# A post-norm transformer layer on one core: four FFN groups walked back and forth, the last block's norm inside the FFN, first loads on two queues

## The reference

```python
q, k, v = (x @ w.T + b).reshape(B, S, 32, 16)        # for wq, wk, wv
scores  = einsum('bshd,bstd->bsht', q, k) / 4          # 32 x 32 for each token
context = einsum('bsht,bstd->bshd', softmax(scores), v)
x = layernorm(x + context)
dq = nf4_dequant(nf4_quant(w))                         # w1, w2 [1376, 512], w3 [512, 1376]
h = silu(x @ dq1.T) * (x @ dq2.T)
x = layernorm(x + h @ dq3.T)
```

## Time and profile before

| what | value |
|---|---|
| median of three executions | 825.99 us |
| profiled execution | 828.94 us, span 827.1 us |
| PE, DVE, ACT, POOL busy | 738.1, 631.5, 469.5, 112.5 us |
| granted clock of TensorE, mean | 0.85 of full speed |
| HBM read, written | 80.55 MB, 38.80 MB |

### The profile page before, as it was taken

The page is one execution under the profiler, slowest core; times in us unless marked ns, Lnnn a source line. Parts: engine busy times, 40 slices in busy tenths (PEclk is TensorE's granted clock), DMA queues, the critical chain, the costliest instruction groups (busy, mean ns, idle before and its releaser), DMA issues.

```text
span 827.1 us, 14113 instructions
## 1 busy us (share of the span) xinstructions
PE 738.1 (89%) x5668; PEld 629.3 (76%) x5668; DVE 631.5 (76%) x844; ACT 469.5 (57%) x599; POOL 112.5 (14%) x91
## 2 busy tenths in 40 slices
...
GB/s 190 248 123 96 189 129 160 138 233 243 252 186 247 139 273 151 246 250 114 189 106 202 81 75 106 178 54 129 69 147 46 140 130 46 102 103 119 85 13 89
DMA packets 88752, 120.27 MB, mean 145 GB/s; under 512 B 24656, under 2 KB 69968, under 8 KB 85616
## 3 DMA queue, kind: packets, MB, share of 16 engines
...
HBM read 80.55 MB, written 38.80 MB: 144 GB/s over the span
## 4 chain that ended last, share of the span: by engine, by line
PE 57%; DVE 23%; issue 9%; ACT 5%; DMA 3%; SPq 1%; ACTq 1%; DVEq 0%
DVE nf_acc L1028 14%; PE ps_p L905 12%; PE ps_p L822 7%; PE ps_p L824 7%; PE ps_p L823 7%; PE ps_s L822 6%; PE ps_s L823 6%; PE ps_s L824 6%; PE ps_s L892 4%; ACT nf_y L666 3%; PE ps_t L843 2%; DMA wst<-in_L_attn_wq 1%; DVE part L1166 1%; SPq L481 1%; DVE f_lb L1046 1%
## 5 line engine op out<-in xcount | busy, mean ns | idle before, releaser
L1028 DVE SCALAR_TENSOR_TENSOR nf_acc<-nf_y,nf_acc 128x1024 f32<-128x1024 f32 (+3 forms) x238 | 298.6, 1255 | 44.0 <-ACT nf_y L666 36.1
L666 ACT ACTIVATE nf_y<-nf_w,bound_b 128x1024 f32<-128x1024 f32 (+3 forms) x255 | 280.8, 1130 | 18.7 <-DVE nf_acc L1028 18.0
L905 PE MATMUL ps_p<-probT,v_bd 128*68 128x32 f32 x1024 | 125.5, 300 | 2.6 <-DVE probT L1077 2.5
L905 PEld LDWEIGHTS ps_p<-probT,v_bd 128*68 128x68 f32 x1024 | 122.6, 211 | 4.1 <-issue 2.6
L822 PE MATMUL ps_s<-x_hl,f_ha 128*128 128x512 f32 (+1 forms) x224 | 88.5, 395 | 0.0
L822 PE MATMUL ps_p<-x_hl,w_hl 128*128 128x512 f32 x192 | 79.2, 412 | 10.0 <-DVE x_hl L1046 8.7
L823 PE MATMUL ps_s<-x_hl,f_ha 128*128 128x512 f32 (+1 forms) x224 | 87.9, 392 | 0.0
L824 PE MATMUL ps_s<-x_hl,f_la 128*128 128x512 f32 (+1 forms) x224 | 87.6, 391 | 0.0
L1191 DVE TENSOR_TENSOR silu<-silu,ps_s 128x512 f32<-128x512 f32 (+1 forms) x44 | 29.9, 680 | 74.8 <-PE ps_s L824 74.7
L809 ACT ACTIVATE hid_hl<-silu 128x512 fp32r<-128x512 f32 (+1 forms) x44 | 27.8, 632 | 86.1 <-DVE silu L1191 85.3
L824 PE MATMUL ps_p<-x_hl,w_hl 128*128 128x512 f32 x192 | 76.5, 399 | 0.0
...
## 6 DMA issues: line engine op xcount, KB each, us to landing
...
```

The costliest lines, as they stand in the source:

```text
L666: act.activation(nf_y[0:p, at % NY, 0:w], nf_w[0:p, u % 2, 0:w], ACT.Identity, bias=bound_b[0:p, i:i + 1], scale=STEEP).then_inc(s_ny, 1)
L905: t = pe.matmul(ps_p[0:MV, (G + 3) % NPV, i * H:(i + 1) * H], v_bd[hb % 2][:, :, g * GI + i], probT[:, G % 2, i], start=True, stop=True)
L1028: dve.scalar_tensor_tensor(out=acc, in0=y, scalar=float(NF4[i + 1]), in1=acc, op0=ALU.min, op1=ALU.max).then_inc(s_nacc, 1)
```

## The change

1. **Groups.** The hidden tiles are four groups of 4, 4, 2 and 1 instead of three of 4, 4 and 3. Odd groups take the blocks 3, 2, 1, 0 (`ORDER`), so at a turn of direction x1 needn't be loaded again (`LOADS`: ten loads instead of twelve). There are 44 steps as before, but 16 stretches of one block instead of 12, each with a drain, and 19 units of dequantisation instead of 17 (285 levels instead of 255); the strips of w3 are narrower for the last two groups (576 and 256 columns for 768). In the last group a block has one step, and `drain` takes the quotient of the norm (`shift_2`) of a quarter while it is at the next.
2. **The end of attention.** The `ct` turns, the norm and the `xt` turns of block 3, and the `f` turns of two `w` units, move from ahead of step 0 into steps 0 to 6.
3. **Levels.** 64 of them instead of 59 in the projections, and in the FFN 3 in a step at first, then 5, 4 and 6, up to step 37; before, 5 in each step up to step 28.
4. **Projections.** x turns one slot earlier, `NV` = 4, and while the projections run turns use four banks (two of `ps_t`, two of `ps_s`).
5. **First loads.** The quarters of wq, wk and wv and the halves of the first x block are issued half by SP, half by ACT, in the order wq, x, wk; the first unit comes behind the biases.

```diff
-    GROUPS = [range(0, 4), range(4, 8), range(8, NJ)]
+    GROUPS = [range(0, 4), range(4, 8), range(8, 10), range(10, NJ)]
+    ORDER = [(g, b if g % 2 == 0 else NBK - 1 - b) for g in range(len(GROUPS)) for b in range(NBK)]
+    for n in range(1, NBL):
+        DRAIN_AT.setdefault(FIRST_STEP[n] + 1, []).append(n - 1)
+    DRAIN_AT.setdefault(NS, []).append(NBL - 1)
-    NQK, NV, NPV = 5, 3, 4
+    NQK, NV, NPV = 5, 4, 4
-    LV_F = [(2, 3)] * (8 * NJG) + [(0, 0)] * (NS - 8 * NJG)
+    LV_F = [(1, 2)] * 4 + [(2, 2)] + [(1, 2)] * 2 + [(2, 3)] * 8 + [(2, 2)] * (FIRST_OF[2] - 15) + [(3, 3)] * 6
+                P_TURNS.setdefault(3 * KC * b + 2 * KC - 1 + c, []).append(("x", b + 1, c))
...
-    TAIL_2 = [("f", u, s) for u in W_UNITS[:1] for s in range(2)]
-    TAIL_3 = [("f", u, s) for u in W_UNITS[1:] for s in range(2)]
-    TURNS += TAIL_1 + TAIL_2 + [("ct", NBK - 1, k) for k in range(len(HEADS))] + TAIL_3
+    TAIL_2 = [("f", u, s) for u in W_UNITS[:2] for s in range(2)]
+    TURNS += TAIL_1 + TAIL_2
+    F_TURNS = {0: [("f", W_UNITS[2], 0), ("f", W_UNITS[2], 1), CT_LAST[0]],
+               1: [("f", W_UNITS[3], 0), ("f", W_UNITS[3], 1), CT_LAST[1]],
+               2: CT_LAST[2:4], 3: CT_LAST[4:], 5: XT_LAST[:2], 6: XT_LAST[2:]}
+    MOMENTS_F, NORM_F = 3, 4
...
         def turn_bank(key):
-            return ps_t[:, TURN[key] % 2]
+            n = TURN[key]
+            if n < NPT:
+                return (ps_t, ps_s)[n % 4 // 2][:, n % 2]
+            return ps_t[:, n % 2]
...
-            load_x(0)
-            load_unit()
+            for q in range(2):
+                load_w(sp, 0, q)
+            load_x(sp, 0, 0)
+            for q in range(2):
+                load_w(sp, 1, q)
             for i, v in enumerate((bq, bk, bv)):
...
+            for q in range(2, Q4):
+                load_w(act, 0, q)
+            load_x(act, 0, 1)
+            for q in range(2, Q4):
+                load_w(act, 1, q)
...
             def turn(key):
                 n = TURN[key]
-                wait(pe, s_tl, n - 1)
+                wait(pe, s_tl, n - 3 if n < NPT else n - 1)
...
                     dve.tensor_tensor(t, ps_p[:, q], t, ALU.add).then_inc(s_drain, 1)
-                    if n >= 2 * NBK:
+                    if n >= LAST_G:
...
                         dve.bn_stats(st6[:, q], t).then_inc(s_bn2, 1)
+                        if q:
+                            shift_2(a - 1, q - 1)
...
+                for m in DRAIN_AT.get(s, []):
+                    drain(m)
...
+                if s == NORM_F:
+                    mean_shift(NBK - 1)
...
+                    if key[0] == "ct":
+                        add_context(key)
+                    else:
+                        low(key)
+                if s == MOMENTS_F:
+                    moments(NBK - 1)
```

More of the change, by code:

```diff
@@ L82, in layer_kernel, with turns_of @@
     NU0 = len(GROUPS[0]) + 2
+    def turns_of(u):
+        kind, g, _ = UNITS[u]
+        return [("f", u, s) for s in range(2 if kind == "w" else -(-len(GROUPS[g]) // 2))]
     def valid(g):
@@ L760, in _ @@
                 i, m = divmod(k, KC)
-                if b == 0 and i < 2:
-                    high(("w", i + 1, m))
-                elif b + 1 < NBK and i == 2:
-                    high(("x", b + 1, m))
+                for key in P_TURNS.get(tau, []):
+                    high(key)
                 if i < 2:
@@ L810, in _ @@
                 for key in F_TURNS.get(s, []):
-                    high(key)
+                    if key[0] != "ct":
+                        high(key)
+                if s == NORM_F:
+                    norm_1(NBK - 1)
                 steep(LV_F[s][1])
-                if g == 2 and b and s == FIRST_STEP[BLOCK_OF[s]] + 1:
-                    for q in range(Q4):
-                        norm_2(b - 1, q)
-            for q in range(Q4):
-                norm_2(NBK - 1, q)
+                for m in DRAIN_AT.get(s, []):
+                    if m >= LAST_G:
+                        for q in range(Q4):
+                            norm_2(m, q)
+            for m in DRAIN_AT[NS]:
+                for q in range(Q4):
+                    norm_2(m, q)
         @block.tensor
@@ L958, in _ @@
                 i, m = divmod(k, KC)
-                if b == 0 and i < 2:
-                    turn(("w", i + 1, m))
-                elif b + 1 < NBK and i == 2:
-                    turn(("x", b + 1, m))
+                for key in P_TURNS.get(tau, []):
+                    turn(key)
                 project(tau)
@@ L977, in _ @@
             for key in TAIL_2:
-                turn(key)
-            for k in range(len(HEADS)):
-                turn(("ct", NBK - 1, k))
-            for key in TAIL_3:
                 turn(key)
```

211 lines of the change are left out of this document (110 added, 101 removed).

## The result

The changed kernel took 798.67 us (median of four runs: 794.23, 795.34, 802.0, 802.1) against 825.93 before, ratio 0.9661 with a 95% interval of 0.9596 to 0.9727. The forecast was 790.3 with a range of 775 to 806: the sign and the range held, but both medians lie outside the 783 to 798 that the forecast gave itself, and the gain was 27 us (24 on the second occasion) and not 36. The profiled execution is one of the longer ones: 802.0 us, span 800.2.

The account below looks back on a forecast made before the run. PE bounds the kernel (busy 738.1 of 827.1 us), so gains lie where it waits: 7.6 + 11 + 9.7 + 13.9 - 6.5 = 35.7 off the median of 825.99 gives 790.3; own range 783 to 798, eight in ten 775 to 806.

Parts of the forecast that it names:

- Start: First loads: wq first on both queues, first projection at about 19 instead of 26.58; gain 7.6 us, bounds 2 and 9.
- The rule of the Trainium skill weighed there: First loads: two issuers save only issue time; as a rival, start gains 1.3 instead of 7.6, 797 us, chance 0.07.
- Token blocks: Projections: x turns one slot earlier shorten PE's waits at new blocks; gain 11 us, bounds 5 and 12.
- The x waits: First projection of blocks 1 to 3: PE waits 2.9 us each for x's last low part; none over 1 us afterwards.
- v_t: End of projections: a fourth buffer ends ACT's wait for a v store; gain 9.7 us, bounds 0 and 9.8.
- The rival: End of projections: SP's issue of the stacks takes over as bound, 9.7 kept back; 800 us, chance 0.06.
- Attention and its end: Attention's pace unchanged, 0; moved turns let the FFN start 15 us earlier, but at the lower clock.
- First FFN steps: FFN steps 0 and 1: waits for third turns, 5 us together, and 1.5 us allowed for the low clock.
- third turns: FFN steps 0 and 1: with two banks the third turn waits 2.5 us for DVE's low part, twice, 5 us.
- Drains: FFN blocks: PE's waits as DVE falls behind with drains and levels; 14.6 us with the clock instead of 24.
- Tail: After the last hidden product: two drains follow instead of one, stores gain 3.1; net 6.5 us later, bounds 3 and 8.

Follow-up runs that it names:

- the second occasion: The changed kernel timed again, unchanged, against the kernel before: 804.1 us (six runs), ratio 0.9718.
- e4: The kernel before with only its first weights and x split over both queues and the first unit behind the biases: 820.73 us, 0.9923.
- e10: The changed kernel with the x turns of the next token block back in their old slots, one later: 815.97 us, 0.9862.
- e3: The kernel before with four v_t buffers and nothing else changed: 824.64 us, 0.998.
- e2: The changed kernel with three v_t buffers again: 803.99 us, 0.9709.
- e1: The changed kernel with POOL waiting for DVE's first level of unit 4 before clearing the second pair of stacks: 796.58 us, 0.9636.
- e5: The changed kernel with the last block's context turns in FFN steps 2 to 4, so no step has three turns: 797.52 us, 0.9642.
- e6: The changed kernel with FFN groups of 4, 4, 1 and 2 and levels spread to suit: 795.63 us, 0.9623.

## Why the forecast was near, and where it failed

- **Start**: right. First turn 8.29 (forecast near 8), first projection 17.80 (near 19); 8.8 us for 7.6, and e4 shows that the loads alone do it. The rule of the Trainium skill weighed there counts issue time only; what moved the start is which bytes come first.
- **Token blocks**: right in kind, 8.7 for 11. The x waits shrank as said, and e10 gives the slot 13.5. What I did not count is a longer wait: PE waits 2.02 and 1.35 us for the low parts of wk and wv (at 32.86 and 49.26), 3.4 us where the kernel before waits 1.3, and the clock from 17 to 60 us is 0.96 where it was 1.00. That DVE is late there by its maximum of unit 0 and its first levels is read from its order and was not tested.
- **v_t**: the step that failed. The forecast gave 9.7 us on the ground that the second stack had a cover of 25 us, "group 8 needs" it. That was a misreading of the code: a half block has four groups (NG is 4), so group 4 needs it, two groups behind group 2 and not six. In e3 the whole kernel gains 2 us, with the wait for the stack in place of v_t's; in the changed kernel it is 0 (e2), because there DVE is held by POOL first, and behind POOL stands the stack (e1). The rival had the right mechanism and got too small a chance, 0.06; its 800 is nearer to what was measured than the 790.3. That POOL could hold DVE stood in no term; the kernel before has a milder case at 181.42, where two levels beside POOL's L587 (180.18 for 2.95 us) take 4.13 us instead of 2.5.
- **Attention and its end**: 18.5 for 15.0. The turns behind attention do as forecast: the first FFN product comes 4.1 us behind the turn that answers to 397.63 (at 376.99), 15.3 less than before. The other 3.2 are luck. PE stood 6.2 us in five places in the kernel before for nothing that the profile names, and 0.9 in two in the changed kernel (rows below), while its waits for `probT` grew from 2.5 to 4.5. The stops lie inside groups, where no instruction waits for another engine; I had taken attention as 0 and do not know their cause. A third of the miss of v_t is covered up by this.
- **First FFN steps**: the third turns wait 2.32 and 2.31 (2.5 forecast). The low clock in the window shown costs 4.2, most of it behind these two waits, where I allowed 1.5; e5 removes both.
- **Drains**: up to step 43 the waits are 5.8 for parts and 5.0 for reloads, 10.7 with rounding, against 12.6 forecast without the clock; the 0.9 named for step 5 was left out of that sum. Block by block they fell elsewhere than said: 1.07 in the second (0.9 forecast), 3.13 in the third (2.0), in the fourth none for a part and 2.37 for a reload (6.5 together), 2.62 for a reload in step 16 (none), none in step 17 (1.5). So the sum is right in part because the errors have both signs.
- **Tail**: right, 6.3 for 6.5: the last hidden product comes 3.2 us behind PE's last `gate_up` (3.4 forecast) and two drains stand behind it, and e6 takes it away by taking one drain away.

PE's waits by line on which the point on attention rests, of the kernel before, then of the changed one (us in total, times, longest):

```profile
PE ps_s L892 <- issue: 6.2, 5, 3.2
```

```profile
PE ps_s L947 <- issue: 0.9, 2, 0.5
```

Not settled, besides: why the same wait of PE is followed by the low clock in some runs and not in others; the two levels of the first occasion, 794 and 802, go with the mean clock, and no experiment here sets it.
